# Conditioning matrices by one-hot products in a fused attention and feed-forward block, with the loads and transposes around them reordered

## What is computed

```python
x = x + attn(cond(x, itok_B_0_30, L0_cond_weights), wq, wk, wv, wo)
x = x + ffn(cond2(x, itok_B_0_7, W, Wr, A, B), up, down, perm)

# cond: w = weights[subjects]   (32 matrices of 32x32)
#       einsum('bct,bcd->bdt', x, w)
# attn: 32 heads of 16, rope, causal mask over 32 positions, softmax, wo
# cond2: base x@W.T plus low-rank experts, top 2 of 8 by a router
# ffn: permute the 512 features, 16 blocks of 32 -> 128 -> gelu -> 32, permute back
```

## Time and profile before

| What | Value |
|---|---|
| Median of 3 runs | 217.81 us (217.02 to 218.19) |
| Profiled execution | 216.94 us |
| Its span in the profile | 215.1 us |
| TensorE busy | 201.6 us, 94% of the span |
| VectorE busy | 147.3 us, 68% |
| GpSimd busy | 122.4 us, 57% |
| ScalarE busy | 114.2 us, 53% |
| DMA | 15.43 MB, mean 72 GB/s |

### The profile page before, as it was taken

The page is one execution under the profiler, slowest core; times in us unless marked ns, Lnnn a source line. Parts: engine busy times, 40 slices in busy tenths (PEclk is TensorE's granted clock), DMA queues, the critical chain, the costliest instruction groups (busy, mean ns, idle before and its releaser), DMA issues.

```text
span 215.1 us, 5966 instructions
## 1 busy us (share of the span) xinstructions
PE 201.6 (94%) x2536; PEld 175.2 (81%) x2536; DVE 147.3 (68%) x283; ACT 114.2 (53%) x189; POOL 122.4 (57%) x96
## 2 busy tenths in 40 slices
PE   4999698699999999999999999999999999798993
PEld 4989675598878999988679899986788987688863
DVE  2368799899488978775646877836769886158223
ACT  2173173692271536439983337289865866533460
POOL 6628996959786201487985201978997344425000
PEclk9999999999999999999999999999999999999999
DMA  6699983300001050000026320000044300134002
GB/s 202 194 375 292 337 282 101 91 11 3 0 3 53 0 186 12 5 0 5 0 27 76 101 97 0 3 0 3 0 52 94 56 5 3 10 38 52 0 3 98
DMA packets 10858, 15.43 MB, mean 72 GB/s; under 512 B 2288, under 2 KB 6544, under 8 KB 10832
## 3 DMA queue, kind: packets, MB, share of 16 engines
q1 hardware_dynamic: 8384, 11.99, 16.8%
q0 software_dynamic: 2160, 3.05, 8.7%
q10 hardware_dynamic: 288, 0.01, 0.1%
HBM read 11.25 MB, written 3.80 MB: 70 GB/s over the span
## 4 chain that ended last, share of the span: by engine, by line
PE 86%; DVE 7%; issue 3%; ACT 2%; DMA 1%
PE ps_A L593 12%; PE ps_A L595 11%; PE ps_A L594 11%; PE ps_F L593 8%; PE ps_F L594 7%; PE ps_F L595 7%; PE ps_S L699 6%; PE ps_F L789 4%; PE ps_A L625 4%; PE ps_S L804 3%; PE ps_S L825 3%; PE ps_S L677 3%; PE ps_A L699 1%; PE ps_A L817 1%; DMA cst<-constants 1%
## 5 line engine op out<-in xcount | busy, mean ns | idle before, releaser
L974 ACT ACTIVATE pbd<-pr 32x512 f32<-32x512 f32 x56 | 35.3, 630 | 5.9 <-DVE pr L1311 5.2
L535 POOL TENSOR_TENSOR pr<-pr,small 128x512 f32<-128x512 f32 x16 | 17.6, 1111 | 35.5 <-DVE small L1305 35.4
L474 POOL TENSOR_TENSOR rot<-rot,cst 128x512 f32<-128x512 f32 x14 | 19.1, 1361 | 15.0 <-DVE rot L1261 14.8
L515 POOL DMA_INDIRECT out<-y,row_at x12 | 19.8, 1646 | 11.3 <-ACT y L974 8.8
L1062 ACT ACTIVATE act<-ps_F 128x512 f32<-128x512 f32 x32 | 16.5, 603 | 11.2 <-PE ps_F L789 11.2
L1283 DVE TENSOR_TENSOR kbd<-kr,cst 128x512 f32<-128x512 f32 x16 | 20.7, 1320 | 2.4 <-POOL kr L478 2.4
L489 POOL TENSOR_TENSOR kbd<-kr,cst 128x512 f32<-128x512 f32 x16 | 20.1, 1283 | 2.1 <-PE ps_F L602 2.0
L593 PE MATMUL ps_A<-xc,wqT 128*128 128x256 f32 x64 | 18.2, 285 | 1.7 <-DVE xc L1229 1.7
L1018 ACT ACTIVATE pr<-pr 128x512 f32<-128x512 f32 x16 | 10.0, 631 | 16.4 <-DVE pr L1297 16.2
L593 PE MATMUL ps_A<-xc,wkT 128*128 128x256 f32 x64 | 18.3, 286 | 0.0
L594 PE MATMUL ps_A<-xc,wkT 128*128 128x256 f32 x64 | 17.9, 279 | 0.0
(11 more groups left out here) (187 smaller groups left out, 614.7 us busy)
## 6 DMA issues: line engine op xcount, KB each, us to landing
xs<-in_x SPq DMA_DIRECT2D x4, 512.0 KB, 6.3
xt<-in_xT SPq DMA_DIRECT2D x4, 512.0 KB, 3.3
out<-xt SPq DMA_DIRECT2D x3, 512.0 KB, 3.0
pbd<-in_L_attn_wq SPq DMA_DIRECT2D x2, 512.0 KB, 4.4
act<-in_L_attn_wk SPq DMA_DIRECT2D x1, 1024.0 KB, 6.2
act<-in_L_attn_wv SPq DMA_DIRECT2D x1, 1024.0 KB, 8.6
act<-in_L_attn_wo SPq DMA_DIRECT2D x1, 1024.0 KB, 10.0
out<-xt SPq DMA_DIRECT2D x2, 256.0 KB, 2.2
```

The costliest lines, as they stand in the source:

```text
L474: pool.tensor_tensor(rv, rv, con("sin").unsqueeze(1).to_broadcast([P, 2 * N // T, T]), ALU.mult).then_inc(rot_sin, 1)
L515: pool.indirect_dma_start(out=out, out_offset=bass.IndirectOffsetOnAxis(ap=row_at[:, g, c:c + 1], axis=0), in_=y[:, c, :], in_offset=None, ...
L535: pool.tensor_tensor(pr[:, i, :, :], pr[:, i, :, :], mx[:, i, :].unsqueeze(2).to_broadcast([P, NH // 2, T]), ALU.mult).then_inc(normed, 1)
L974: return sc.activation(dst, src, ACT.Copy)
```

## The change

**Conditioning matrices.** The conditioning weights now come with the constants, laid out in four groups of 32 partitions (256 more columns). VectorE compares the subject numbers, sent for 128 columns, with the partition's own number, which gives one-hot columns. TensorE multiplies: `select(r)` makes four products of 32 rows by 32 columns against 256 columns, four times, into the four banks of ring F. VectorE transposes each bank in blocks of 32 into `wsel` (`turn_selected`), from which the blocks of all groups are made. The three gathers, the write to HBM and the read back are gone, and with them `idx`, `wg`, `rows` and SyncE's waits for them.

**Loads.** x of group 0 is issued by ScalarE's queue. wq comes as a quarter, a quarter and a half, and its high and low parts are made in quarters. The w2 gathers are issued once wq has landed. The raw slices lie in both `xt` buffers, in `y` and in the third buffer of `vz`; xt of groups 0 and 1 is loaded once the last w2 transposition is done.

**Rings.** The first conditioning goes into A and S together and is split by column halves. Q and K of group 0 go into ring F (`QK`), Q with the contraction step as the outer loop (`first_q`).

**Order.** 2, 4 and 2 warm-up products in place of 16 and 6. The w2 transposes move behind the first scores, the last behind Q of group 1. ScalarE makes the K blocks of three of the four chunks of tile 1 (`k_blocks(c)`). GpSimd clears the third `vz` buffer after the last w2 transposition. On VectorE the maxima of group 0 come ahead of the low halves of w2, and both first ropes of group 1 come ahead of sums(0, 2).

The core of the diff:

```diff
+            def select(r):
+                it = Fi("sel", r)
+                rows = slice(T * r, T * r + T)
+                for j in range(BT):
+                    at = slice(T * j, T * j + T)
+                    last = pe.matmul(bank(it)[at, 0:SC * T], onehot[rows, at], wst[rows, :],
+                                     start=True, stop=True, skip_group_check=True)
+                last.then_inc(s_full(it), 1)
...
+            def turn_selected(r):
+                it = Fi("sel", r)
+                wait_full(ve, it)
+                ve.transpose(wsel[:, SC * r:SC * r + SC, :].rearrange("p d t -> p (d t)"),
+                             bank(it)[:, 0:SC * T]).then_inc(s_free(it), 1)
...
+            def first_q():
+                its = [QK(0, i) for i in range(2)]
...
+                for k in range(KC):
+                    wait_w(pe, "wq", k + 1)
+                    if k % 2 == 0:
+                        for r in range(2):
+                            wait_read(pe, first_cond(k // 2, r))
```

On ScalarE:

```diff
+            def k_blocks(c):
+                wait_rope(sc, 0, 2 + c // 2)
+                kv = kr[:, c, P:2 * P].rearrange("p (b s) -> p b s", b=BT)
+                for h in range(HG):
+                    last = sc.activation(kbd[:, 1, c, :, T * h:T * h + T], kv, ACT.Copy,
+                                         scale=con("head")[:, h:h + 1])
+                last.then_inc(kbd_a, 1)
```

Where the raw slices of w2 lie:

```diff
-        raw_w2b = [xt[:, 1, :, :].rearrange("p c n -> p (c n)")[:, 0:WB]] + [kbd1[:, WB * c:WB * c + WB]
-                                                                            for c in range(KC - 1)]
+        raw_w2b = [xt[:, r, :, :].rearrange("p c n -> p (c n)")[:, 0:WB] for r in range(2)] + [
+            y_flat[:, 0:WB], vz[:, 2, :, :].rearrange("p a b -> p (a b)")[:, 0:WB]]
```

On SyncE:

```diff
             sp.dma_start(cst[:, :], consts).then_inc(d_cst, 16)
-            load_x(0)
-            sp.dma_start(raw["wq"][:, 0:2, :], wq_rows[:, 0:2, :]).then_inc(d_w["wq"], 16)
-            sp.wait_ge(d_wg[0], 16)
+            sp.dma_start(raw["wq"][:, 0:1, :], wq_rows[:, 0:1, :]).then_inc(d_w["wq"], 16)
+            sp.dma_start(raw["wq"][:, 1:2, :], wq_rows[:, 1:2, :]).then_inc(d_wq1, 16)
             sp.dma_start(raw["wq"][:, 2:4, :], wq_rows[:, 2:4, :]).then_inc(d_wq2, 16)
-            sp.wait_ge(d_wg[1], 16)
             load_w("wk")
             load_w("wv")
```

On GpSimd:

```diff
-            pool.wait_ge(d_w["wk"], 16)
+            pool.wait_ge(d_wq2, 16)
             perm_rows()
...
                 if more:
                     norm(g, 0)
                     norm(g, 1)
                 if g == 0:
+                    wait_full(pool, prep("w2", KC - 1))
+                    pool.memset(vz[:, 2, :, :], 0.0).then_inc(vz_zero, 1)
                     wo_los()
                 if more:
                     rope(g + 1, 0)
```

On TensorE:

```diff
             pe.wait_ge(d_cst, 16)
-            idle_products(16)
-            cond(0, 0)
-            cond(0, 1)
-            idle_products(6)
...
+            idle_products(2, rings["S"][0])
+            pe.wait_ge(onehot_ready, 1)
+            for r in range(BT):
+                select(r)
+            idle_products(4, rings["S"][0])
+            first_conds()
+            idle_products(2, rings["F"][3])
+            first_q()
+            qk(0, "wk", 0)
+            qk(0, "wk", 1)
+            v(0, 0)
+            v(0, 1)
+            scores(0, 0)
             pe.wait_ge(d_w["w2b"], 16 * KC)
-            for k in range(KC - 1):
-                prep_w2(k)
-            prep_b()
-            wait_w(pe, "wv")
-            v(0, 0)
-            scores(0, 0)
-            prep_w2(KC - 1)
-            v(0, 1)
+            prep_w2(0)
+            prep_w2(1)
             cond(1, 0)
             cond(1, 1)
+            prep_w2(2)
+            prep_b()
             scores(0, 1)
...
                 if g == 0:
+                    prep_w2(KC - 1)
                     pv(0, 0, 0)
```

On VectorE, ahead of the loop over groups:

```diff
             w_los("wk", raw["wk"], WT["wk"], 2)
+            w_los("wv", raw["wv"], WT["wv"], 2, (0,))
             rope(0, 0)
             rope(0, 1)
-            w_los("wv", raw["wv"], WT["wv"], 2, (0,))
             rope(0, 2)
             w_los("wv", raw["wv"], WT["wv"], 2, (1,))
             rope(0, 3)
             k_blocks(0, 0, 2)
             k_blocks(0, 0, 3)
-            w2_los(0)
             max_shift(0, 0)
             max_shift(0, 1)
-            k_blocks(0, 1, 2)
-            k_blocks(0, 1, 3)
+            cond_lo(1, 0)
+            cond_lo(1, 1)
             sums(0, 0)
             sums(0, 1)
-            w2_los(1)
-            cond_lo(1, 0)
+            w2_los(0)
             turn(0, 0)
-            cond_lo(1, 1)
             turn(0, 1)
```

On VectorE, group 0:

```diff
-                    w2_los(2)
                     max_shift(0, 2)
+                    rope(1, 0)
                     max_shift(0, 3)
-                    split_lo(prep("b"), bT[:, 0, :], bT[:, 1, :], prep_hi, KC)
-                    rope(1, 0)
+                    rope(1, 1)
                     sums(0, 2)
                     sums(0, 3)
-                    w2_los(3)
-                    rope(1, 1)
+                    w2_los(1)
                     turn(g, 2)
                     turn(g, 3)
+                    w2_los(2)
                     rope(1, 2)
+                    split_lo(prep("b"), bT[:, 0, :], bT[:, 1, :], prep_hi, KC)
+                    w2_los(3)
                     blocks(2)
                     rope(1, 3)
```

More of the change, by code:

```diff
@@ L446, in _ @@
         def _(pool):
[L447 to L461, removed]
+            pool.memset(vz[:, 0:2, :, :], 0.0).then_inc(vz_zero, 1)
             def perm_rows():
@@ L611, in prep_b, with first_conds @@
                 last.then_inc(s_full(it), 1)
+            def select(r):
[6 more added lines that the diff above has]
+                last.then_inc(s_full(it), 1)
+            def first_conds():
+                pe.wait_ge(d_x[0], 16)
+                pe.wait_ge(wbd_ready, 1)
+                for c in range(KC):
+                    for t in range(GT):
+                        for r in range(2):
+                            it = first_cond(c // 2, r)
+                            rows = slice(P // 2 * r, P // 2 * r + P // 2)
+                            at = P * (c % 2) + P // 2 * t
+                            last = pe.matmul(bank(it)[:, at:at + P // 2], xs[rows, 0, t, P * c:P * c + P],
+                                             wbd[rows, t, :, :], start=True, stop=True, skip_group_check=True)
+                            if t == GT - 1 and c % 2:
+                                last.then_inc(s_full(it), 1)
             def cond(g, t):
                 pe.wait_ge(d_x[g], 16)
-                pe.wait_ge(wbd_ready, g + 2 if g else t + 1)
+                pe.wait_ge(wbd_ready, g + 1)
                 its = [A(g, COND + r) for r in range(2)]
@@ L628, in cond, with qk @@
                             last.then_inc(s_full(it), 1)
-            def qk(g, name, first, i):
+            def first_q():
+                its = [QK(0, i) for i in range(2)]
+                for it in its:
+                    wait_free(pe, it)
+                W = WT["wq"]
+                for k in range(KC):
+                    wait_w(pe, "wq", k + 1)
+                    if k % 2 == 0:
+                        for r in range(2):
+                            wait_read(pe, first_cond(k // 2, r))
+                    for i, it in enumerate(its):
+                        for h in range(2):
+                            c = 2 * i + h
+                            last = mm3(bank(it)[:, N * h:N * h + N],
+                                       W[:, 0, k, P * c:P * c + P], W[:, 1, k, P * c:P * c + P],
+                                       xc[:, 0, k, :], xc[:, 1, k, :], h == 0 and k == 0, h == 1 and k == KC - 1,
+                                       skip=True)
+                        if k == KC - 1:
+                            last.then_inc(s_full(it), 1)
+            def qk(g, name, i):
                 W = WT[name]
@@ L1442, in _ @@
                                ).then_inc(mask_ready, 1)
-            ve.wait_ge(d_permc, 16)
+            for r in range(BT):
+                turn_selected(r)
+            blocks(0)
             step(ve.tensor_copy(permf, permc[:, :]))
@@ L1614 @@
         give(f"in_{name}", given[name])
-    give("constants", constants())
+    give("constants", np.concatenate([constants(), given["L0_cond_weights"]], axis=1))
     give("columns", np.broadcast_to(np.arange(D, dtype=np.float32), (P, D)))
-    args.append(nc.dram_tensor("rows", (B, T * T), F32, kind="Internal").ap())
     args.append(nc.dram_tensor("out_0", (G * D, N), F32, kind="ExternalOutput").ap())
```

248 lines of the change are left out of this document (134 added, 114 removed).

## The result

The changed kernel took 221.32 us in the median of four executions (220.22 to 222.38), the kernel before 217.71 on the same chip: a ratio of 1.017, 95% interval 1.010 to 1.024. Slower, as forecast; 220.2 was forecast, and 217.4 to 222.6 as the range. In both sets two executions lie at 220.2 to 220.5 and two at 221.9 to 222.6.

What follows compares the result with a forecast made beforehand. Bound: TensorE's own chain and the rope chain through VectorE and GpSimd, level at V of group 1. T 6.0 us earlier, 9.0 lost behind it: 2.95 later, added to 216.94 and 217.81, forecast 220.2; range 217.4 to 222.6.

Steps and rivals of the forecast that it cites:

- T: Start of Q of group 1 on TensorE: forecast at 36.8 us, 6.0 earlier than 42.85.
- From T on: Behind Q of group 1: GpSimd's new wait delays the ropes, V at T+22.9 instead of T+13.9, 9.0 us lost.
- the first term: GpSimd ahead of wo: waiting for the last w2 transposition before clearing vz costs 3 us of idle time.
- the second: GpSimd's norms: sums(0,2) stands behind rope(1,1) on VectorE, so the norms come behind a rope, costing 2.4 us.
- From rope(0,0) to T: Group 0's ropes, first scores and group 1's conditioning: from 17.7 to 37.1 us, with GpSimd free of gathers.
- The head: Start up to the first Q: conditioning takes 1.96 us, Q starts at about 10.3, 3.2 us earlier than 13.51.
- rival (d): Head: fewer warm-up products leave Q at half clock for its whole 5.7 us; T = 40.7, 224 us; chance 0.08.
- wv's landing: Loads in the head: wv lands at 15.4 us and rope(0,0) waits for it, starting at 17.7.
- A first Q at up to 12 costs nothing: Group 0's Q, complete at 16.0, may be as late as 17.7, when rope(0,0) starts.
- Selection: Head: 16 one-hot products of 32x32 against 256 columns on TensorE, 1.1 us, doubled for the slow clock to 2.2.
- (b): Rival: group 0's ropes don't wait for wv, TensorE alone sets T at 32.8; 216.7 us; chance 0.11.
- (c): Rival: level, T between 32.8 and 34.9 by earlier wv and undisturbed VectorE halves; 217.8 to 218.2 us; chance 0.13.

Runs made afterwards that it cites:

- e1: Changed kernel with GpSimd making wo's low halves before the w2 wait, wait and vz clearing moved behind rope(1,1): 216.93 us, ratio 0.992.
- e2: Changed kernel with VectorE's rope(1,1) moved behind group 0's two sums, sums(0,2) and sums(0,3): 216.47 us, ratio 0.990.
- e3: Changed kernel with both reorderings, wo ahead of the wait and sums ahead of rope(1,1): 212.29 us, ratio 0.971.
- e4: Kernel before with one added GpSimd wait, for the end of Q of group 1 ahead of wo: 223.43 us, ratio 1.021.
- e11: e1 with 12 unread products on TensorE ahead of V of group 1: 214.33 us, ratio 0.982.
- e10: The changed kernel unaltered, run again in a later set on the second chip: 221.11 us, ratio 1.012.
- e12: e3 unaltered, run again in a later set on the second chip: 212.39 us, ratio 0.973.
- e9: e3 with four first warm-up products in place of two: 212.69 us, ratio 0.975.
- e7: e3 with eight first products and VectorE's rope(0,0) and rope(0,1) ahead of wv's first low half: 221.05 us, ratio 0.997.

## Why the prediction was right, and where it was not

**From T on: right.** The wait for the last w2 transposition (T+6.4 forecast, clearing at T+6.42), wo to T+11.84, second K half at T+15.9, V at T+22.94. e1 took out the first term (4.4 us of V's start), e2 and e3 the second, e4 put the first into the kernel before. The step that the forecast left out is the clock behind the hole: it costs nothing in the changed kernel, where a second wait follows, 0.7 in e2, where K holds V up, and 2.2 to 2.4 us in e1, where V itself is slow (e11).

**From rope(0,0) to T: right.** 19.5 us, as 17.7 to 37.1 was worked out, and 25.6 before. First scores to T: 5.3, forecast 5.2. The stretch became 6.1 us shorter, as forecast from GpSimd free of the gathers and VectorE free of the late w2 halves. That is read from the trace; no run puts either of them back, so how the 6 us divide between them, the K blocks on ScalarE and the moved transpositions isn't shown.

**The head: the step that failed.** "The conditioning 1.96 ... gives Q at about 10.3" took the duration of a warm engine behind eight warm-up products instead of 22. In the profiled execution it took 3.7 (8.56 to 12.24) and Q started at 13.04. The part ahead of it was off too: the conditioning began at 8.56, not 7.5. I had this as rival (d), a late clock, at 0.08, with T = 40.7; it came in part, T = 39.05. By the traces at hand the head has two outcomes:

| | Q of group 0 | rope(0,0) starts | T |
|---|---|---|---|
| forecast | 10.3 | 17.7 | 36.8 |
| late clock (after, e2, e3, e10) | 12.9 to 13.0 | 19.4 to 20.2, waits for Q | 38.9 to 39.7 |
| early clock (e1, e11, e12) | 10.8 to 11.0 | 16.2 to 16.7, behind wv's low half | 35.7 to 36.1 |

With an early clock rope(0,0) starts right behind wv's low half, as forecast, 1.0 to 1.5 us earlier. But wv's landing, which I had as the cause, holds it in one trace only. wv landed at 14.1 (e1) and 14.4 (e12), not 15.4, and in e1, e9 and e11 VectorE goes from wk's halves to wv's without a wait: there its own row of work sets rope(0,0). In e12 the landing costs 0.42 us, and one can read the chain, ScalarE then VectorE:

```profile
14.41 2.01 ACT L1029 ACTIVATE wvT<-act 128x1024 fp32r<-128x1024 f32 x2 [0.77 <-DMA act<-in_L_attn_wv]
```
```profile
15.51 1.23 DVE L1294 TENSOR_TENSOR wvT<-act,wvT 128x1024 fp32r<-128x1024 f32 x1 [0.42 <-ACT wvT L1029]
```

With a late clock Q is the later of the two: VectorE waits 1.7 us for it in the changed kernel. A late conditioning delays VectorE itself as well: it is done with wv's half at 17.89 there and at 16.4 in e1, for the low parts of the conditioned x stand ahead of wk's. "A first Q at up to 12 costs nothing" did not hold either: e9's Q starts at 11.67, 0.85 behind e12's, and rope(0,0) and T come 0.3 later. So that the T of the forecast, 36.8, fell between the two outcomes, and 220.2 near the median, was luck as far as the head goes. It forecast 2.95 us of loss against 5.2 in the profiled executions, and the difference is T, at 39.05 and not 36.8.

**Selection.** 2.2 us was forecast, 1.15 measured (5.22 to 6.36 with its weights). The scores' rows gave 1.1 at the full clock, and I doubled that for the half clock; the weight loads on either side take 0.33, so it took half of what I forecast for that clock. Four full products of 128 columns take 1.78 us of weight loads in the same stretch, 0.45 each; sixteen of 256 columns one after the other would by that be 14 us, so by this estimate twelve or so ran at once. The Trainium skill, "TensorEngine Tiling (Array Packing)", Theoretical Speedup, allows up to 16 where both dimensions are 32 or less, and the trace's twelve lie within that. Between selection and conditioning the transposes and blocks took 2.2, not 0.9.

**The clock.** The same head here had the full clock from 8.5 us on in some executions and from 15.9 to 17.4 in others. The Trainium skill, "TensorE: Matmul & The Clock Gate", The HAM clock gate, says of matmuls issued back to back that the moment at which the clock rises varies from run to run, by some 0.5 us. The measurement decides: in this head, whose products are not back to back, it is seven to nine microseconds. Whether the little work ahead of the conditioning is the reason isn't shown.

**The rivals.** (b) and (c) asked for T below 34.9; the earliest seen is 35.7, so neither came. Their prices were not taken from one base: V 0.35 us later gives 217.3 on the profiled 216.94, where (c) has 217.8, and V 1.05 earlier gives 215.9, where (b) has 216.7. The net: 6.0 us gained up to T by the forecast, 3.8 in the profiled execution, 9.0 lost behind it.

## What to carry to other kernels

When a buffer is lent to another job, look at what is queued behind the wait that takes it back: here a 0.74 us memset held wo, a rope and a norm, and moving it, with one rope moved behind two small sums, turned +1.2% into -2.7% (e10, e12). When a change shortens the chain at one point, write out the other chain from there; here the 3.8 us gained up to T were real, and more than all of them was lost in the next 23. A hole in TensorE's work can cost more than its length if what follows is on the path. Behind the holes of 3.8 to 4.5 us here (changed kernel, e1, e2, e4) the clock fell to half each time; behind those of 0.7 to 1.3 us ahead of K and V in e3, e9, e11 and e12 it did not (the three short waits of e7 are the exception). For a hole as long as the former, price the next group of products at half the clock, or fill it with products for which nobody waits.

## What was not expected of the hardware

- The same head, on the same chip, had TensorE's weight loads at 0.19 us from 8.4 us on in e11 and e12 and not before 17 us in e10; on the other chip it was so from 8.5 in e1 and from 17.4 in e3. The time differs by 3 to 4 us (212.1 against 216.0 in e3).
- The granted clock reads 1.00 in the head, where the weight loads show half of it, but 0.50 behind the hole, where they show the same. The durations are the surer sign.
- Waits of under a microsecond each, in a stretch in which TensorE was busy for 2.17 of 4 us, were followed by nine microseconds at 0.50 (e7), though the engine was busy throughout.
- The kernel before took 217.7, 218.4, 219.9 and 218.0 us in four sets of runs, the last two on one chip; so below 1% only ratios within a set tell anything.
